# A chain of four networks in one program: value products of the last attention in column tiles, probabilities turned inside V's product, and the router's mean in column tiles

## The chip, the cores and the metric

The kernel runs on one core of one Trainium2 chip. The core has a matrix engine (PE, with its weight loads shown apart as PEld), a vector engine (DVE), a scalar engine (ACT), a general one (POOL) and SP, which here only issues transfers. Each engine works through its own list of instructions in order and waits on semaphores for the others. The metric is the device time of one execution in microseconds; three runs of the kernel before gave 366.67, 365.13 and 364.26, median 365.13.

## The reference

128 nodes with 768 features go through four layers, each a graph network and a feed-forward part. The change lies in the last feed-forward part, a small transformer block with a router. What matters of it, with x of 128 x 768 (here B = 1, N = 128):

```python
HEADS = 12; HD = 64; RHD = 512; RANK = 256
e = _gelu(_ln(x, r_ln_g, r_ln_b) @ r_in_w.T + r_in_b)
g = jnp.mean(e[:, RESERVE:, :], axis=1, keepdims=True)
f = jnp.concatenate([e, jnp.broadcast_to(g, e.shape)], axis=-1)
h1 = _gelu(f @ r_o1_w.T + r_o1_b)
h2 = _gelu(h1 @ r_o2_w.T + r_o2_b)
logits = (h2 @ r_o3_w.T + r_o3_b).reshape(B, N, BS, 2)
...
xa = _ln(x, ln1_g, ln1_b)
q = (xa @ wq.T + bq).reshape(B, N, HEADS, HD).transpose(0, 2, 1, 3)
...
s = jax.nn.softmax(jnp.einsum('bhqd,bhkd->bhqk', q, k) / np.float32(np.sqrt(HD)), axis=-1)
o = jnp.einsum('bhqk,bhkd->bhqd', s, v).transpose(0, 2, 1, 3).reshape(B, N, DIM)
o = o @ wo.T + bo
h = x + bits[:, :, 0:1] * o
```

Each node's router input is its own 512 features beside the mean of all nodes (the first one left out), so r_o1 is a product over 1024, of which the second 512 are the same for every node. Everything is float32.

## The kernel before

The program is written engine by engine; the order on each engine is the order of the code, and semaphores (wait_ge, then_inc) tie the engines together. Weights come through a ring of eight slots of 128 x 4608, each a unit that SP loads ahead; all units of the last part (r_in, wq, r_o1, wk, wv, wo, down, up) are such units. PSUM is one tensor of eight banks of 512 columns; bank(n, w, off) names w columns of bank n.

A product on PE is mm(out, stationary, moving): the stationary operand (up to 128 x 128) is loaded as weights and the moving one is streamed. In float32 each product shows in the trace as two passes, each a weight load and a MATMUL; a transposition tr is one pass. With tile_position a product uses only some rows or columns of the array: (0, 32 t) or (0, 64 n) is a column tile, whose output lies in 32 or 64 of the 128 partitions of PSUM. Two places of the kernel before use column tiles: L1724 (four tiles of 32 columns) and L1841 (join_mlp, two of 49). The scores at L1908 use two row tiles, one for the even heads (features 0 to 63 of a chunk), one for the odd ones.

The last block on PE runs in this order. product_T multiplies transposed activations: for each output chunk o of 128 it adds products over the input chunks c, all at L1862. First r_in (stationary weights, moving xT), four output chunks, each passed by ACT through GELU into h1[:, 0:512] (features on partitions, nodes in columns). Then q's product. Meanwhile DVE sums h1 over the nodes into gmean, 128 x 4. Then r_o1: per output chunk four products with the nodes' chunks of h1 and four with a column of gmean that is broadcast over 128 columns (node_or_mean); outputs alternate between banks 6 and 7, chunk o from the third on waits for the GELU of chunk o - 2, which ACT writes to h1[:, 512:1024] (L673). Then k's product, r_o2, and V's product (L1918): first the wide half, columns 0 to 511, then the narrow one, 512 to 767, six chunks each; behind the first chunk stand the router's logits (L1902) and the twelve score products (L1908).

During V's product DVE takes the maxima of the scores by groups of four heads (L1292), ACT takes the exponentials of twelve heads (L684), and DVE scales each group with one over its sum (L1298), which gives p_ready 1, 2 and 3. POSITION orders the heads. Then PE turns the twelve 128 x 128 probability blocks into banks 4, 5 and 3 (L1927), ACT copies each group to h2 (L495, pT_ready), DVE adds the bias to all of V at once into g4 (L1302, v_ready) and makes the residual g3 (L1305). A head's value product (L1935) has 128 stationary columns, that is both heads of a chunk of V, so that half of each output is not used:

```python
last = mm(ps[:, h * P:(h + 1) * P], g4[:, (h // 2) * P:(h // 2 + 1) * P], h2[:, at * P:(at + 1) * P],
          start=True, stop=True)
```

Even heads are taken from partitions 0 to 63 of the output by ACT (L495), odd ones from 64 to 127 by DVE (L1310), each in two pieces, into xT. The output projection (L1946) waits for both engines' first pieces, later for the second ones. Behind it come the residual (L1313), statistics, and the rest of the block.

## Time and profile before

| | us |
|---|---|
| Median of three runs | 365.13 |
| Span of the profiled execution | 362.7 |
| PE busy | 349.9 |
| DVE busy | 180.6 |
| ACT busy | 66.3 |
| r_o1, from its first pass to the first of k's product | 7.14 |
| From the end of V's product to the output projection | 4.19 |

The span goes from the first to the last instruction; the run's time also has what lies around it. The chain that ended last follows the work back from the last instruction to whatever released it; PE makes 84% of it. In a timeline, rows of one line that follow each other are put together with a count, and the time of such a row goes from its first start to its last end, where the end of a MATMUL is modelled and includes the way out of the array; passes that follow each other start closer together than they last.

### The profile page before, as it was taken

How to read it: one execution, taken by the hardware profiler on the slowest of the kernel's cores; microseconds unless marked ns; L12 is line 12 of the kernel's file. 1: busy time of each engine (PE TensorE's matmuls, PEld its weight loads, DVE VectorE, ACT ScalarE, POOL GpSimd, SP SyncE). 2: the span in 40 equal slices, each digit the busy share in tenths (PEclk: the TensorE clock that was granted, in tenths of full speed). 3: DMA queues.
4: the chain of work that ended last, by engine and by line, in shares of the span. 5: the costliest groups of instructions: out<-in, count | busy, mean ns of one | idle time of the engine just before them, and what ended most of it. 6: DMA issues, size and time to landing. Idle time of an engine off the chain costs nothing.

```text
span 362.7 us, 4277 instructions
## 1 busy us (share of the span) xinstructions
PE 349.9 (96%) x1633; PEld 222.1 (61%) x1633; DVE 180.6 (50%) x547; ACT 66.3 (18%) x154; POOL 38.4 (11%) x62
## 2 busy tenths in 40 slices
PE   7999999999999999999899999999999799999997
PEld 3466666656565656655556556564555599967754
DVE  4846337485838475467644835325642301163441
ACT  2002101101011111012012220024133401064010
POOL 4900000010000002041040000041030100000000
PEclk9999999999999999999999999999999999999999
DMA  8999999998854949999985375794371600000001
GB/s 279 416 379 429 428 416 427 424 380 303 345 230 149 414 149 418 413 408 414 382 376 192 136 272 213 260 354 161 150 276 28 275 2 3 0 2 0 2 0 43
DMA packets 10502, 90.19 MB, mean 249 GB/s; under 512 B 2169, under 2 KB 2822, under 8 KB 6386
## 3 DMA queue, kind: packets, MB, share of 16 engines
q1 hardware_dynamic: 8238, 84.91, 59.2%
q0 software_dynamic: 848, 3.61, 2.9%
q10 hardware_dynamic: 1396, 1.40, 1.1%
q8 instruction: 13, 0.21, 0.2%
q14 instruction: 7, 0.06, 0.0%
HBM read 89.53 MB, written 0.39 MB: 248 GB/s over the span
## 4 chain that ended last, share of the span: by engine, by line
PE 84%; DVE 8%; DMA 3%; issue 1%; SPq 1%; ACT 1%; POOL 1%; DVEq 0%; ACTq 0%
PE ps L1491 15%; PE ps L1457 14%; PE ps L1862 8%; PE ps L1436 6%; PE ps L1664 4%; PE ps L1683 4%; DMA ring<-in_gat_w 3%; PE ps L1479 3%; PE ps L1774 2%; PE ps L1946 2%; PE ps L1918 2%; PE ps L1966 2%; PE ps L1557 2%; DVE stats L716 1%; PE ps L1498 1%; PE ps L1368 1%
## 5 line engine op out<-in xcount | busy, mean ns | idle before, releaser
L1457 PE MATMUL ps<-ring,xT 128*128 128x512 f32 (+1 forms) x168 | 56.6, 486 | 0.9 <-DMA ring<-in_gat_w 0.9
L1491 PE MATMUL ps<-ring,h 128*128 128x512 f32 (+1 forms) x168 | 55.6, 486 | 0.0
L1491 PEld LDWEIGHTS ps<-ring,h 128*128 128x128 f32 x168 | 31.2, 190 | 21.9 <-issue 20.1
L1457 PEld LDWEIGHTS ps<-ring,xT 128*128 128x128 f32 x168 | 30.8, 191 | 20.0 <-issue 16.9
L782 DVE CUSTOM_DVE_ANT_0 g<-h,avec 128x768 f32<-128x768 f32 x8 | 7.7, 959 | 35.9 <-ACT h L495 22.8
L495 ACT ACTIVATE h<-ps 128x768 f32<-128x768 f32 (+6 forms) x24 | 13.6, 577 | 60.2 <-PE ps L1457 16.2
L1436 PE MATMUL ps<-ring,xT 128*128 128x512 f32 (+1 forms) x72 | 24.0, 487 | 0.0
L870 DVE TENSOR_SCALAR ring<-ring,idxb,ewb 128x128 bf16<-128x128 bf16 x99 | 22.5, 309 | 0.0
L1368 PE MATMUL ps<-shiftm 128*128 128x512 bf16 x66 | 19.4, 418 | 3.1 <-POOL shiftm L386 2.1
L380 POOL TENSOR_TENSOR rstd<-var,mhalf 128x1 f32<-128x1 f32 x8 | 4.6, 579 | 144.1 <-DVE var L724 69.3
L1436 PEld LDWEIGHTS ps<-ring,xT 128*128 128x128 f32 x72 | 13.4, 190 | 9.0 <-issue 8.1
L1683 PE MATMUL ps<-ring,h 128*128 128x512 f32 (+1 forms) x48 | 16.4, 492 | 0.0
L1862 PE MATMUL ps<-g,ring 128*128 128x128 f32 x144 | 16.4, 275 | 0.0
L1862 PEld LDWEIGHTS ps<-g,ring 128*128 128x128 f32 x144 | 16.2, 192 | 0.0
L1664 PE MATMUL ps<-ring,xT 128*128 128x384 f32 x48 | 16.0, 488 | 0.0
L495 ACT ACTIVATE xT<-ps 128x256 f32<-128x256 f32 (+2 forms) x18 | 7.1, 395 | 39.9 <-PE ps L1384 28.1
L1368 PEld LDWEIGHTS ps<-shiftm 128*128 128x128 bf16 x66 | 6.5, 110 | 12.5 <-issue 4.5
L1683 PEld LDWEIGHTS ps<-ring,h 128*128 128x128 f32 x48 | 8.8, 190 | 6.5 <-issue 6.1
L920 DVE TENSOR_TENSOR x<-ps,xb 128x512 f32<-128x512 f32 (+1 forms) x8 | 4.4, 553 | 16.7 <-PE ps L1436 13.4
L536 ACT ACTIVATE g<-g 128x768 f32<-128x768 f32 x8 | 6.7, 843 | 31.7 <-DVE g L816 31.7
L527 ACT ACTIVATE att<-att,soft 128x128 f32<-128x128 f32 x9 | 3.6, 402 | 48.5 <-DVE soft L799 48.5
L1261 DVE TENSOR_TENSOR g<-ps,cols 128x768 f32<-128x768 f32 x2 | 1.9, 958 | 20.9 <-PE ps L1862 20.9
(394 smaller groups left out, 512.7 us busy)
## 6 DMA issues: line engine op xcount, KB each, us to landing
ring<-in_gat_w SPq DMA_DIRECT2D x15, 2304.0 KB, 11.3
avec<-in_gat_a SPq DMA_DIRECT2D x9, 768.0 KB, 10.2
ring<-in_l_w SPq DMA_DIRECT2D x3, 2304.0 KB, 15.6
ring<-in_gat_w SPq DMA_DIRECT2D x6, 384.0 KB, 6.4
ring<-in_l_w SPq DMA_DIRECT2D x2, 1152.0 KB, 12.8
ring<-in_l1f_w1a SPq DMA_DIRECT2D x1, 2304.0 KB, 12.9
ring<-in_l1f_w1b SPq DMA_DIRECT2D x1, 2304.0 KB, 9.8
ring<-in_l1f_w2a SPq DMA_DIRECT2D x1, 2304.0 KB, 11.1
```

Of the source, the lines that this page charges most:

```text
L495: return nc.scalar.activation(dst, src, ACT.Copy)
L782: link(nc.vector.tensor_tensor_reduce(g3[:], hp, avec[:, 0:D], 1.0, 0.0, ALU.mult, ALU.add, alpha[:, par, 0:1]))
L870: last_ = nc.vector.tensor_scalar(oh_src[:, 1 + k, e, :], iotab, idxb[:, 1, e:e + 1], ewb[:, k, e:e + 1], ALU.is_equal, ALU.mult)
L1368: mm(bank(spare), some[:, 0:P], some[:, 0:WIN], start=True, stop=True)
L1436: last = mm(ps[:, at + lo:at + hi], xT[:, c, :], w[:, c, lo:hi], start=(c == 0), stop=(c == C - 1))
L1457: last = mm(ps[:, at + lo:at + hi], xT[:, c, :], w[:, c, lo:hi], start=(c == 0), stop=(c == C - 1))
L1479: last = mm(ps[:, 6 * WIN + c * P:6 * WIN + (c + 1) * P], h1[:, par * D + c * P:par * D + (c + 1) * P], attnT[:, par, :], start=True, stop ...
L1491: last = mm(ps[:, 4 * WIN + lo:4 * WIN + hi], h2[:, par * D + c * P:par * D + (c + 1) * P], w[:, c, lo:hi], start=(n == 0 and c == 0), sto ...
L1557: last = mm(ps[:, 4 * WIN + lo:4 * WIN + hi], h2[:, D + c * P:D + (c + 1) * P], w[:, c, lo:hi], start=False, stop=(c == C - 1))
L1664: last_ = mm(bank(g, H0), xT[:, c, :], weights[:, c, lo:lo + H0], start=(c == 0), stop=(c == C - 1))
L1683: last_ = mm(ps[:, lo:hi], h2[:, g * H0 + c * P:g * H0 + (c + 1) * P], weights[:, 3 * (g % 2) + c, lo:hi], start=False, stop=(g == 3 and c ...
L1862: last_ = mm(to, weights[:, c, o * P:(o + 1) * P], operand(c), start=(c == 0), stop=(c == chunks - 1))
```

## The change

In the router's r_o1, the mean's product is no longer repeated for 128 columns in each of four output chunks. Four column tiles of 32 take one column of gmean each as stationary operand (broadcast over 32 columns), with 512 columns of r_o1's weights moving, into the four quarters of bank 0: tile t's rows all hold chunk t's share of the mean's row. ACT copies bank 0, scaled by 1/32, to h2[:, 0:512] (mean_rows), and per output chunk one product of mean_rows with ones adds the sum over all 128 partitions to the four node products.

In the attention, the twelve turns of probabilities move into V's product, four after the wide half, four in the middle of the narrow half, four after it. V's bias is added in two instructions, one per half, with the residual's g3 between them. A head's value product has 64 stationary columns, and the two heads of a chunk go to two column tiles, so that a chunk's output lies as the projection needs it, on 128 partitions. Three copies of 128 x 256 take the place of four of 64 partitions: ACT, DVE, ACT.

```diff
+        mean_rows = h2[:, 0:RHD]
...
@@ ACT
+            act.wait_ge(s("mean_ps"), 1)
+            nc.scalar.activation(mean_rows, bank(0), ACT.Copy, scale=1.0 / BIT).then_inc(s("mean_copied"), 1)
             for f in range(4):
                 act.wait_ge(s("ro1_ps"), f + 1)
...
             for g in range(3):
                 act.wait_ge(s("pT_ps"), g + 1)
                 copy(h2[:, g * 512:(g + 1) * 512], bank((4, 5, 3)[g])).then_inc(s("pT_ready"), 1)
-            o_ps = ps[:, 0:AH * P].rearrange("p (c b n) -> p c b n", b=2, n=P)
-            for n, (lo, hi) in enumerate(((0, 4), (4, C))):
+            for n in (0, 2):
                 act.wait_ge(s("oT_ps"), n + 1)
-                copy(xT[0:AD, lo:hi, :], o_ps[0:AD, lo:hi, 0, :]).then_inc(s("o_even_ready"), 1)
+                copy(xT[:, 2 * n:2 * n + 2, :], bank(n, 2 * P).rearrange("p (c n) -> p c n", n=P)) \
+                    .then_inc(s("o_outer_ready"), 1)
...
@@ DVE
-            dve.wait_ge(s("v_ps"), 1)
+            def heads_values(n):
+
+                lo, hi = HALVES[n]
+                dve.wait_ge(s("v_ps"), n + 1)
+                nc.vector.tensor_tensor(g4[:, lo:hi], ps[:, 6 * WIN + lo:6 * WIN + hi], avec[:, D + lo:D + hi], ALU.add) \
+                    .then_inc(s("v_ready"), 1)
+
             dve.wait_ge(s("in_bv"), 16)
-            nc.vector.tensor_tensor(g4[:], ps[:, 6 * WIN:6 * WIN + D], avec[:, D:2 * D], ALU.add).then_inc(s("v_ready"), 1)
-
+            heads_values(0)
             dve.wait_ge(s("in_bo"), 16)
             link(nc.vector.scalar_tensor_tensor(out=g3[:], in0=avec[:, 0:D], scalar=bit[:, 0:1], in1=xn[:], op0=ALU.mult,
                                                 op1=ALU.add))
-            o_ps = ps[:, 0:AH * P].rearrange("p (c b n) -> p c b n", b=2, n=P)
-            for n, (lo, hi) in enumerate(((0, 4), (4, C))):
-                dve.wait_ge(s("oT_ps"), n + 1)
-                nc.vector.tensor_copy(xT[AD:P, lo:hi, :], o_ps[AD:P, lo:hi, 1, :]).then_inc(s("o_odd_ready"), 1)
+            heads_values(1)
+            dve.wait_ge(s("oT_ps"), 2)
+            nc.vector.tensor_copy(xT[:, 2:4, :], bank(1, 2 * P).rearrange("p (c n) -> p c n", n=P)) \
+                .then_inc(s("o_inner_ready"), 1)
...
@@ PE
-            product_T(unit(U_RO1, "r_o1", "p (c n) -> p c n", c=8), 6, 4, node_or_mean, "ro1_ps", emptied="h1T_ready")
+            w = unit(U_RO1, "r_o1", "p (c n) -> p c n", c=8)
+            for t in range(4):
+                last = mm(ps[t * BIT:(t + 1) * BIT, 0:RHD], gmean[:, t:t + 1].broadcast_to([P, BIT]), w[:, 4 + t, :],
+                          start=True, stop=True, tile_position=(0, t * BIT))
+            last.then_inc(s("mean_ps"), 1)
+            for o in range(4):
+                if o >= 2:
+                    pe.wait_ge(s("h1T_ready"), o - 1)
+                for c in range(4):
+                    mm(bank(6 + o % 2, P), w[:, c, o * P:(o + 1) * P], h1[:, c * P:(c + 1) * P], start=(c == 0), stop=False)
+                if o == 0:
+                    pe.wait_ge(s("mean_copied"), 1)
+                mm(bank(6 + o % 2, P), mean_rows[:, o * P:(o + 1) * P], ones[:], start=False, stop=True) \
+                    .then_inc(s("ro1_ps"), 1)
...
+            def turn_probabilities(g):
+
+                pe.wait_ge(s("p_ready"), g + 1)
+                for h in range(4):
+                    last_ = tr(bank((4, 5, 3)[g], P, h * P), h1[:, (4 * g + h) * P:(4 * g + h + 1) * P], ident)
+                last_.then_inc(s("pT_ps"), 1)
...
                     if lo == 0 and c == 0:
                         scores()
+                    if lo > 0 and c == 2:
+                        turn_probabilities(1)
+                last.then_inc(s("v_ps"), 1)
+                if lo == 0:
+                    turn_probabilities(0)
+            turn_probabilities(2)
...
+            def out_at(c):
+
+                return bank(c // 2, P, c % 2 * P)
+
+            def heads_out(c):
+
+                for half in range(2):
+                    at = POSITION[2 * c + half]
+                    last_ = mm(out_at(c)[half * AD:(half + 1) * AD],
+                               g4[:, c * P + half * AD:c * P + (half + 1) * AD], h2[:, at * P:(at + 1) * P],
+                               start=True, stop=True, tile_position=(0, half * AD))
+                return last_
 
             pe.wait_ge(s("v_ready"), 1)
+            pe.wait_ge(s("pT_ready"), 2)
+            for c in range(C):
+                if c == 4:
+                    pe.wait_ge(s("v_ready"), 2)
+                    pe.wait_ge(s("pT_ready"), 3)
+                last = heads_out(c)
+                if c % 2:
                     last.then_inc(s("oT_ps"), 1)
             wait_unit(pe, U_O)
...
                     if lo == 0 and c in (0, 4):
-                        pe.wait_ge(s("o_even_ready"), 1 + c // 4)
-                        pe.wait_ge(s("o_odd_ready"), 1 + c // 4)
+                        pe.wait_ge(s("o_outer_ready"), 1 + c // 4)
+                    if lo == 0 and c == 2:
+                        pe.wait_ge(s("o_inner_ready"), 1)
```

The order on PE at r_o1, before. A row is a line, the operation, out<-in, the output's shape and a count; in the brackets stand the semaphores that it waits for. The names in it: h is h1 (the nodes' features), cells is gmean, ring the weights.

```order
L1862 MATMUL ps<-h,ring 128x128 [waits gmean_ready,slot3_in]
L1862 MATMUL ps<-h,ring 128x128 x3
L1862 MATMUL ps<-cells,ring 128x128 x4
L1862 MATMUL ps<-h,ring 128x128 x4
L1862 MATMUL ps<-cells,ring 128x128 x4
L1862 MATMUL ps<-h,ring 128x128 [waits h1T_ready]
L1862 MATMUL ps<-h,ring 128x128 x3
L1862 MATMUL ps<-cells,ring 128x128 x4
L1862 MATMUL ps<-h,ring 128x128 [waits h1T_ready]
L1862 MATMUL ps<-h,ring 128x128 x3
L1862 MATMUL ps<-cells,ring 128x128 x4
```

After the change, the same place; here h at L1907 is h2 (mean_rows).

```order
L1897 MATMUL ps<-ring,cells 32x512 [waits gmean_ready,slot3_in]
L1897 MATMUL ps<-ring,cells 32x512 x3
L1904 MATMUL ps<-h,ring 128x128 x4
L1907 MATMUL ps<-ones,h 128x128 [waits mean_copied]
L1904 MATMUL ps<-h,ring 128x128 x4
L1907 MATMUL ps<-ones,h 128x128
L1904 MATMUL ps<-h,ring 128x128 [waits h1T_ready]
L1904 MATMUL ps<-h,ring 128x128 x3
L1907 MATMUL ps<-ones,h 128x128
L1904 MATMUL ps<-h,ring 128x128 [waits h1T_ready]
L1904 MATMUL ps<-h,ring 128x128 x3
L1907 MATMUL ps<-ones,h 128x128
```

The sixteen products with the mean are gone from between the node products; the four with 512 columns stand ahead of them, and one product per output chunk behind.

The order on PE from the end of V's wide half through the value products, before: h at L1927 is h1 (probabilities), at L1935 it is h2 (turned probabilities), and g is g1 or g4 (V).

```order
L1918 MATMUL ps<-ring,g 128x256 x6
L1927 MATMUL ps<-shiftm,h 128x128 [waits p_ready]
L1927 MATMUL ps<-shiftm,h 128x128 x3
L1927 MATMUL ps<-shiftm,h 128x128 [waits p_ready]
L1927 MATMUL ps<-shiftm,h 128x128 x3
L1927 MATMUL ps<-shiftm,h 128x128 [waits p_ready]
L1927 MATMUL ps<-shiftm,h 128x128 x3
L1935 MATMUL ps<-h,g 128x128 [waits pT_ready,v_ready]
L1935 MATMUL ps<-h,g 128x128 x3
L1935 MATMUL ps<-h,g 128x128 [waits pT_ready]
L1935 MATMUL ps<-h,g 128x128 x3
L1935 MATMUL ps<-h,g 128x128 [waits pT_ready]
```

After the change:

```order
L1934 MATMUL ps<-shiftm,h 128x128 [waits p_ready]
L1934 MATMUL ps<-shiftm,h 128x128 x3
L1942 MATMUL ps<-ring,g 128x256 x3
L1934 MATMUL ps<-shiftm,h 128x128 [waits p_ready]
L1934 MATMUL ps<-shiftm,h 128x128 x3
L1942 MATMUL ps<-ring,g 128x256 x3
L1934 MATMUL ps<-shiftm,h 128x128 [waits p_ready]
L1934 MATMUL ps<-shiftm,h 128x128 x3
L1961 MATMUL ps<-h,g 64x128 [waits pT_ready,v_ready]
L1961 MATMUL ps<-h,g 64x128 x7
L1961 MATMUL ps<-h,g 64x128 [waits pT_ready,v_ready]
L1961 MATMUL ps<-h,g 64x128 x3
```

The twelve turns, which stood behind V's narrow half, stand in three places, and the value products wait twice instead of three times, for two signals each.

The order on DVE at the same place, before and then after the change (g is g4, then g3; cells holds sums and bits).

```order
L1298 TENSOR_TENSOR h<-h,cells 128x512 [waits dve_step]
L1302 TENSOR_TENSOR g<-ps,avec 128x768 [waits in_bv,v_ps]
L1305 SCALAR_TENSOR_TENSOR g<-avec,cells,xn 128x768 [waits in_bo]
L1310 COPY xT<-ps 64x512 [waits oT_ps,dve_step]
L1310 COPY xT<-ps 64x256 [waits oT_ps]
L1313 SCALAR_TENSOR_TENSOR g<-ps,cells,g 128x512 [waits wo_ps]
```

```order
L1302 TENSOR_TENSOR h<-h,cells 128x512 [waits dve_step]
L1308 TENSOR_TENSOR g<-ps,avec 128x512 [waits v_ps,in_bv]
L1314 SCALAR_TENSOR_TENSOR g<-avec,cells,xn 128x768 [waits in_bo]
L1308 TENSOR_TENSOR g<-ps,avec 128x256 [waits v_ps,dve_step]
L1318 COPY xT<-ps 128x256 [waits oT_ps]
L1322 SCALAR_TENSOR_TENSOR g<-ps,cells,g 128x512 [waits wo_ps]
```

V's bias is two instructions with g3 between them, and one copy of 128 partitions stands where two of 64 stood.

## Rows read from the trace of the kernel before

**Rows 1.** The page: span, busy us of each engine, PE's granted clock by slices.

```profile
span 362.7 us, 4277 instructions
...
PE 349.9 (96%) x1633; PEld 222.1 (61%) x1633; DVE 180.6 (50%) x547; ACT 66.3 (18%) x154; POOL 38.4 (11%) x62
...
PEclk9999999999999999999999999999999999999999
```

**Rows 2.** Chain that ended last, from 299.9 us: start us, us, what.

```profile
299.90 17.42 PE ps L1862 x156
...
318.52 1.54 PE ps L1908 x24
320.06 7.08 PE ps L1918 x22
327.14 1.31 PE ps L1927 x12
328.45 2.82 PE ps L1935 x24
...
331.33 7.99 PE ps L1946 x24
...
352.35 7.76 PE ps L1436 x24
```

**Rows 3.** The same chain, earlier: passes of 384 columns, and L1841's second piece.

```profile
207.39 3.87 PE ps L1664 x12
...
283.21 1.45 PE ps L1841 x8
```

**Rows 4.** Timeline of PE at the two column-tiled lines: start us, us, line, count.

```profile
234.85 2.16 PE L1724 MATMUL ps<-ring,h 128*32 128x192 f32 x48
...
279.40 2.79 PE L1841 MATMUL ps<-ring,h 128*49 128x384 f32 x16
```

**Rows 5.** Timeline of PE's weight loads at L1841.

```profile
279.40 0.17 PEld L1841 LDWEIGHTS ps<-ring,h 128*49 128x49 f32 x4 [0.33 <-issue]
279.77 0.13 PEld L1841 LDWEIGHTS ps<-ring,h 128*49 128x49 f32 x2 [0.19 <-issue]
280.09 0.13 PEld L1841 LDWEIGHTS ps<-ring,h 128*49 128x49 f32 x2 [0.19 <-issue]
```

**Rows 6.** Timeline of PE over r_o1: the first piece of each kind.

```profile
300.19 1.06 PE L1862 MATMUL ps<-h,ring 128*128 128x128 f32 x8
301.08 1.06 PE L1862 MATMUL ps<-cells,ring 128*128 128x128 f32 x8
```

**Rows 7.** Groups by line and shape, 225 to 363 us: busy us, mean ns.

```profile
L495 ACT ACTIVATE xT<-ps 128x256 f32<-128x256 f32 x8 | 3.1, 384 | 18.7 <-PE ps L1384 10.3 <-PE ps L1951 6.8 <-PE ps L1828 1.6
...
L495 ACT ACTIVATE h<-ps 128x512 f32<-128x512 f32 x3 | 1.6, 598 | 2.6 <-PE ps L1927 2.6
```

**Rows 8.** Timeline of ACT: first GELU of r_o1, end of the last exponential.

```profile
302.17 0.37 ACT L673 ACTIVATE h<-ps,cols 128x128 f32<-128x128 f32 x1 [9.46 <-PE ps L1862]
...
324.70 0.27 ACT L684 ACTIVATION_READ_ACCUMULATOR h<-ps,cells 128x1 f32 x1
```

**Rows 9.** Timeline of DVE: first and last of three scalings, g3, copies.

```profile
322.42 0.69 DVE L1298 TENSOR_TENSOR h<-h,cells 128x512 f32<-128x512 f32 x1
...
325.21 0.69 DVE L1298 TENSOR_TENSOR h<-h,cells 128x512 f32<-128x512 f32 x1
...
328.06 1.01 DVE L1305 SCALAR_TENSOR_TENSOR g<-avec,cells,xn 128x768 f32<-128x768 f32 x1
330.49 1.25 DVE L1310 COPY xT<-ps 64x512 f32<-64x512 f32 x2 [1.42 <-PE ps L1935]
```

**Rows 10.** Instructions of L1841 and L1862: ns min/median/max, first and last start.

```profile
L1841 PEld LDWEIGHTS ps<-ring,h x24: 120/124/124, 279.4 to 283.8; 128*49 128x49 f32 x24
L1841 PE MATMUL ps<-ring,h x24: 486/486/524, 279.4 to 284.1; 128*49 128x384 f32 x24
...
L1862 PEld LDWEIGHTS ps<-g,ring x144: 191/192/192, 292.0 to 315.2; 128*128 128x128 f32 x144
```

More of the change, by code:

```diff
@@ L1921, in _ @@
                         scores()
-            last.then_inc(s("v_ps"), 1)
-            pT_banks = (4, 5, 3)
-            for g in range(3):
-                pe.wait_ge(s("p_ready"), g + 1)
-                for h in range(4):
-                    last = tr(bank(pT_banks[g], P, h * P), h1[:, (4 * g + h) * P:(4 * g + h + 1) * P], ident)
-                last.then_inc(s("pT_ps"), 1)
-            pe.wait_ge(s("v_ready"), 1)
-            for at in range(AH):
-                h = POSITION.index(at)
-                if at % 4 == 0:
-                    pe.wait_ge(s("pT_ready"), at // 4 + 1)
-                last = mm(ps[:, h * P:(h + 1) * P], g4[:, (h // 2) * P:(h // 2 + 1) * P], h2[:, at * P:(at + 1) * P],
-                          start=True, stop=True)
-                if at in (7, 11):
+                    if lo > 0 and c == 2:
[13 more added lines that the diff above has]
+                return last_
+            pe.wait_ge(s("v_ready"), 1)
+            pe.wait_ge(s("pT_ready"), 2)
[5 more added lines that the diff above has]
+                if c % 2:
                     last.then_inc(s("oT_ps"), 1)
```

2 lines of the change are left out of this document (removed).

## The prediction

> **What bounds the kernel now.** I read the page's shares first: PE is busy 96% of the span, and PEclk stays at 9 in all forty slices, which is the 2.4 GHz level [rows 1]. Then the chain that ended last, from 299.9 us on: one PE line begins where the one before ends, to within 0.06 us, and no transfer and no other engine stands between them up to the end of the output projection [rows 2]. So both places of the change lie on the chain, and a microsecond of PE saved there is a microsecond of the span, as long as no copy becomes late.
>
> Three prices come out of the chain. A float32 product takes two passes, each a weight load and a MATMUL. A pass with 128 moving columns costs 17.42 / 156 = 0.1117 us, a transposition (one pass) 1.31 / 12 = 0.109 [rows 2]. A pass with 384 columns costs 3.87 / 12 = 0.3225 us [rows 3], or 0.84 ns per column, which makes 0.43 for 512 and 0.215 for 256. Check: 12 x 0.43 + 12 x 0.215 = 7.74, and the last product takes 7.76 [rows 2].
>
> **Column tiles in the trace of before.** Two lines already use them. L1841 has two tiles of 49 columns: 16 passes of 384 columns take 2.79 us from the first start to the modelled end [rows 4]. Alone they would take 16 x 0.3225 = 5.2. The weight loads show the pattern: two of them every 0.32 us, one full-width slot [rows 5]. L1724 has four tiles of 32 columns: 48 passes of 192 columns in 2.16 us [rows 4], where 12 sets of 0.161 make 1.94 and 48 single passes would make 7.7. So both two and four tiles run side by side, and a set costs as much as one pass.
>
> Going in and out of tiles is not free. Scores (row tiles, 12 pairs, 128 columns) take 1.54 us where 12 x 0.1117 = 1.34, so 0.20 to enter. The V product behind them takes 7.08, where 10 wide and 12 narrow passes make 6.88, so 0.20 to leave [rows 2]. L1841's second piece, 8 passes or 4 sets, takes 1.45 instead of 1.29: 0.16 to enter with narrow tiles [rows 3].
>
> **The change part by part.**
>
> *Router's mean.* Removed: 16 products against the broadcast mean, 32 passes in four pieces of 8 [rows 6], 32 x 0.1117 = 3.57 us. Added: four tiles with 512 columns, two sets of 0.43 = 0.86; entering 0.15 and leaving 0.20; four products of the copied mean rows with the ones, 8 x 0.1117 = 0.89. Together 2.10, so 1.47 is saved. Bounds: the two sets cost 0.86 if four tiles run side by side (L1724) and 8 x 0.43 = 3.44 if they don't; I take 0.86, since L1724 has the same number of tiles and the same 32 columns, and only its moving width differs.
>
> New on ACT is one copy of 128x512 from PSUM; the nearest row says 598 ns [rows 7]. PE waits for it before the ones' product of the first output chunk. From the start of the tiles' last set: 0.60 until its modelled end (a MATMUL of 384 lasts 486 ns [rows 10], 0.165 more than its slot, so 0.43 + 0.165), 0.04 hand-over, 0.60 copy, 0.04 back: 1.28. PE meanwhile streams 0.43, leaves the tiles 0.20 and does eight node passes 0.89: 1.52. The copy is hidden with 0.24 to spare. If it isn't, each tenth is a tenth of the span. Behind the copy on ACT stand the four GELUs of r_o1; the first is wanted by the third chunk, ten passes (1.12) after its product ended, and takes 0.37 [rows 8].
>
> *Value products.* Before, from 328.45 to the start of L1946 at 331.33: 2.88 us for 24 passes, with a small wait at the front and one for the copies at the end [rows 2]. After: 12 sets of two tiles with 64 weight columns. Bounds for a set: 0.109 (the transposition's slot) below, 2 x 0.1117 = 0.223 above if the pair takes turns. No row has two column tiles of 64 columns and a moving width of 128. The nearest are the scores, paired by rows at that width, and L1841, paired by columns at three times the width; in both a pair costs one slot, so I take 0.1117. 12 x 0.1117 + 0.17 to enter = 1.51; leaving falls into L1946, which takes 7.99 now against 7.76 for an unhindered product [rows 2], so it already pays about what leaving costs. Saved: 2.88 - 1.51 = 1.37.
>
> *Transpositions inside V.* Nothing is removed: 12 x 0.109 stay on PE in three groups of four. Their purpose is the copies behind them. I laid the new order on the clock of before (as if the router's part were unchanged). V's wide half ends about 324.45 (320.06 + 5 x 2 x 0.43, and some delay at its start); the first group needs p_ready 1, given when DVE's first scaling ends at 323.1; the three scalings stand 1.39 us apart [rows 9]. So it doesn't wait, and ends at 324.9. Three narrow chunks (6 x 0.215) end at 326.2, the second group (p_ready 2: 324.5) at 326.6, three more chunks at 327.9, the third group (p_ready 3: 325.9) at 328.35. ACT is through with the exponentials at 324.97 [rows 8], copies the first group by 325.6, the second by 327.4, and the third (ready 0.2 after its last slot) by 329.2. DVE adds bias to V's wide half from 325.9 to 326.6 (0.69, as its other pass over 128x512), makes g3 (1.01) until 327.7, and adds bias to the narrow half (ready at about 328.1) by 328.6 [rows 9].
>
> PE's first four head pairs need V's wide half (326.6) and copies 1 and 2 (327.4), and run from 328.5 to 329.4; the last two need the narrow half (328.6) and copy 3 (329.2), and run to 329.85. The margin is 0.2 us, the smallest of this part; without it each tenth that ACT is late is a tenth of the span. Results leave in three copies of 128x256, 0.38 each on ACT [rows 7] and about as much on DVE: the first, behind copy 3, is done at 329.6, the second on DVE at about 330.0, the third on ACT at 330.5. The output projection takes them at 329.85, four wide passes later (331.7) and eight later (333.4). None is late. The half-height copies of before, DVE's two of them at 330.49 [rows 9], which ended after the last value product, disappear from the path.
>
> **The sum.** 1.47 + 1.37 = 2.84 us. The profiled execution's span is 362.7; the runs have a median of 365.13, 2.4 more, which I take as what lies around the span and leave unchanged. So the span becomes 359.8 and the time 362.3 us, 0.8% less. A difference of about 1% is what a measurement of this kernel can tell from none: its three times lie between 364.26 and 366.67.
>
> **The rivals.**
>
> A. The pair of 64-column tiles takes turns at 128 columns: a set costs 0.223, the value products 2.7 + 0.2, and their part is nothing. Only the mean pays: 365.13 - 1.47 = 363.7. For it: no row has this form, and each set must load 128 weight columns within 0.11 us. Against it: the scores load two sets of 128 columns per slot and lose nothing.
>
> B. A new wait takes part of the gain: the mean's copy (margin 0.24) or the third copy of the probabilities (0.2). If ACT needs half a microsecond more at both, 0.6 comes back: 362.9. For it: both margins are small; against it: ACT has no other work at the mean's place, where it was idle for 9.46 us before the first GELU [rows 8].
>
> C. Slower: column tiles take turns at both places, and a pass's weight load isn't covered by the pass before. A load lasts 124 ns for 49 columns and 192 for 128 [rows 10], so about 137 for 64 and 110 for 32. Values: 24 x (0.137 + 0.112) + 0.17 = 6.15, 3.3 more than now; mean: 8 x (0.110 + 0.43) + 0.35 + 0.89 = 5.56, 2.0 more; in all 370.4. Turns alone already raise the mean's two sets from 0.86 to 3.44, and the whole is 1.1 us slower (366.2). Each part alone turns to a loss once a set of four costs over 1.17 us, a pair over 0.226. Against it: at L1841's start four loads lie within 0.17 us [rows 5], so the second pair loads while the first pair's matmuls, 486 to 524 ns long [rows 10], run. The Trainium skill states this rule ("TensorE: Matmul & The Clock Gate", Part 3, The mechanism): a weight load overlaps running matmuls only if its row group differs, which it doesn't among column tiles; by that rule the time would be C's. The trace disagrees: at L1841 and L1724 all passes use the same 128 rows, and a set still costs one slot.
>
> D. More than the sum: entering and leaving cost nothing (L1927 follows L1918 without a gap) and a pair's slot is 0.109, 0.55 us more: 361.7.
>
> **How the numbers follow.** The forecast 0.66, A 0.10, B 0.12, C 0.04, D 0.08. The likeliest is 362.3; A and B reach up to 363.7, D down to 361.7, and the median of a few runs of this kernel may lie half a microsecond off: 361.0 to 363.9. Faster by over 1% means below 361.5: a fifth of the forecast (scatter) and half of D, 0.18; C holds 0.04, of which a quarter (turns with covered loads) is within 1%, so slower has 0.03; the rest, 0.79, is within 1%.
>
> **What would show it.** In the profile after, the chain should stay on PE. The line of the four-tile mean should have 8 passes, whose weight loads come in two groups of four, 0.43 to 0.46 us apart; the stretch from the end of q's product to the first K pass should shrink from 64 x 0.1117 = 7.15 to about 5.7; the value products' 24 passes should take about 1.5 in the chain, and the output projection should start 0.05 us behind them without a wait. PE idle before the ones' product (on ACT's copy) shows B, as does idle before the fifth head pair; pairs 0.22 apart show A. I would be wrong most likely in the price of entering and leaving tiles, which I know only as a difference of sums.

## The result, and the profile after

The changed kernel takes 362.44 us (median of six runs, 361.21 to 363.22), the kernel before beside it 364.84 (six runs, 364.26 to 366.67). The ratio is 0.9927, with a 95% interval of 0.9904 to 0.995: a gain of 0.7%, about what was forecast, and within the 1% at which the chances were drawn. The profiled execution took 362.13 us with a span of 360.3; before, the span was 362.7 [rows 1].

The page of the changed kernel: the span, and busy us of each engine.

```profile
span 360.3 us, 4241 instructions
...
PE 346.4 (96%) x1612; PEld 217.9 (60%) x1617; DVE 180.2 (50%) x547; ACT 66.8 (19%) x155; POOL 38.3 (11%) x62
```

The chain that ended last, from r_o1 on: start us, us, what. L1897 is the four-tile mean, L1904 the node products, L1907 the products of the mean rows with ones, L1942 V, L1934 the turns, L1961 the value products, L1983 the output projection; L1871 is product_T.

```profile
300.93 0.99 PE ps L1897 x8
301.92 1.09 PE ps L1904 x8
303.01 0.22 PE ps L1907 x2
303.24 0.89 PE ps L1904 x8
...
306.59 9.83 PE ps L1871 x88
...
319.15 4.49 PE ps L1942 x10
323.64 0.44 PE ps L1934 x4
324.08 1.30 PE ps L1942 x6
...
327.55 1.46 PE ps L1961 x24
329.01 7.95 PE ps L1983 x24
```

One PE line begins where the one before ends, as in [rows 2]. No row of ACT or DVE has come in between, so none of the new copies is late. The value products take 1.46 us where L1935 took 2.82. The same stretch as a timeline of PE (start us, time to the modelled end of the last pass, line, stationary and moving operand, shape, count):

```profile
300.86 1.06 PE L1897 MATMUL ps<-ring,cells 128*32 128x512 f32 x8
301.85 1.16 PE L1904 MATMUL ps<-h,ring 128*128 128x128 f32 x8
...
306.42 8.20 PE L1871 MATMUL ps<-g,ring 128*128 128x128 f32 x72
...
319.08 4.56 PE L1942 MATMUL ps<-ring,g 128*128 128x512 f32 x10
...
327.48 1.53 PE L1961 MATMUL ps<-h,g 128*64 128x128 f32 x24
328.94 8.01 PE L1983 MATMUL ps<-ring,xT 128*128 128x512 f32 x24
```

Two stretches can be read from first starts, which are not modelled, and they serve as yardsticks below. The **r_o1 stretch**, from its first pass to k's first, is 300.86 to 306.42, 5.56 us; before it was 7.14. The **V stretch**, from V's restart behind the scores to the output projection, is 319.08 to 328.94, 9.86 us; before it ran from 319.99 to 331.33, 11.34. That is 1.58 and 1.48 us less. Of the first, 0.09 is given back ahead of it: in the trace of single instructions the first tile's pass starts 0.20 us behind q's last pass, where passes that follow each other at this width stand 0.11 apart. Net 1.49 + 1.48 = 2.97 us, against 2.84 in the sum. From the two spans only 2.4 is gone: r_in, which lies ahead of all that the change touches, began 0.58 us later in this execution (287.29, before 286.71), and 2.97 - 0.58 = 2.39. The experiments come back to this.

### The profile page after: what moved, and what is told of

Read it like the earlier page. It is cut to its first block, busy times and chain, and to the rows that moved or that the text cites. A ratio compares the mean times of both kernels' runs of the same rounds, so it can differ in the third digit from the quotient of the medians.

```text
span 360.3 us, 4241 instructions
## 1 busy us (share of the span) xinstructions
PE 346.4 (96%) x1612; PEld 217.9 (60%) x1617; DVE 180.2 (50%) x547; ACT 66.8 (19%) x155; POOL 38.3 (11%) x62
## 4 chain that ended last, share of the span: by engine, by line
PE 80%; DMA 10%; DVE 5%; SPq 2%; issue 1%; ACT 1%; POOL 1%; DVEq 0%; ACTq 0%
PE ps L1500 15%; PE ps L1466 14%; PE ps L1445 7%; PE ps L1871 7%; DMA ring<-in_l_wu 6%; PE ps L1673 4%; PE ps L1692 4%; DMA ring<-in_gat_w 3%; PE ps L1488 3%; PE ps L1783 2%; PE ps L1983 2%; PE ps L1942 2%; PE ps L2003 2%; PE ps L1566 2%; DVE stats L720 2%; PE ps L1507 1%
## 5 line engine op out<-in xcount | busy, mean ns | idle before, releaser
L1466 PEld LDWEIGHTS ps<-ring,xT 128*128 128x128 f32 x168 | 30.8, 191 | 20.3 <-issue 16.9
L1377 PE MATMUL ps<-shiftm 128*128 128x512 bf16 x61 | 17.8, 412 | 3.6 <-POOL shiftm L388 2.1
L1445 PEld LDWEIGHTS ps<-ring,xT 128*128 128x128 f32 x72 | 13.4, 190 | 9.0 <-issue 8.1
L1871 PE MATMUL ps<-g,ring 128*128 128x128 f32 x144 | 16.4, 275 | 0.0
L1871 PEld LDWEIGHTS ps<-g,ring 128*128 128x128 f32 x144 | 16.2, 192 | 0.0
L497 ACT ACTIVATE xT<-ps 128x256 f32<-128x256 f32 x18 | 6.9, 383 | 38.5 <-PE ps L1393 27.9
L1673 PEld LDWEIGHTS ps<-ring,xT 128*128 128x128 f32 x48 | 8.9, 190 | 5.6
```

Source lines behind the costliest of these rows:

```text
L497: return nc.scalar.activation(dst, src, ACT.Copy)
L1377: mm(bank(spare), some[:, 0:P], some[:, 0:WIN], start=True, stop=True)
L1445: last = mm(ps[:, at + lo:at + hi], xT[:, c, :], w[:, c, lo:hi], start=(c == 0), stop=(c == C - 1))
L1466: last = mm(ps[:, at + lo:at + hi], xT[:, c, :], w[:, c, lo:hi], start=(c == 0), stop=(c == C - 1))
L1673: last_ = mm(bank(g, H0), xT[:, c, :], weights[:, c, lo:lo + H0], start=(c == 0), stop=(c == C - 1))
L1871: last_ = mm(to, weights[:, c, o * P:(o + 1) * P], operand(c), start=(c == 0), stop=(c == chunks - 1))
```

## The experiments

e1 to e8 were to tell which part earns what, and why; w1 to w4 came of the scatter in their times. Line numbers differ by a few from kernel to kernel. Kernels with a single run are read by the two stretches, not by the time.

### e1 and e2: each part alone

e1 has the mean in column tiles and the attention of before:

```diff
-            product_T(unit(U_RO1, "r_o1", "p (c n) -> p c n", c=8), 6, 4, node_or_mean, "ro1_ps", emptied="h1T_ready")
+            w = unit(U_RO1, "r_o1", "p (c n) -> p c n", c=8)
+            for t in range(4):
+                last = mm(ps[t * BIT:(t + 1) * BIT, 0:RHD], gmean[:, t:t + 1].broadcast_to([P, BIT]), w[:, 4 + t, :],
+                          start=True, stop=True, tile_position=(0, t * BIT))
...
```

> The kernel before with the router's mean in four column tiles and nothing else. My theory: the two parts of the change are independent, each pays what its own stretch of PE shows. From the first pass of r_o1 to the first of k's product 5.56 us as after (7.14 before); from V's wide half (first pass behind the scores) to the output projection 11.34 as before; time 1.5 us below the kernel before, about 363.3. Rival (the parts share a cover, so that one alone pays little): less than 1 us gained.

e2 has the attention of the change and the mean of before (the same lines the other way round):

```diff
-            for t in range(4):
-                last = mm(ps[t * BIT:(t + 1) * BIT, 0:RHD], gmean[:, t:t + 1].broadcast_to([P, BIT]), w[:, 4 + t, :],
-                          start=True, stop=True, tile_position=(0, t * BIT))
...
+            product_T(unit(U_RO1, "r_o1", "p (c n) -> p c n", c=8), 6, 4, node_or_mean, "ro1_ps", emptied="h1T_ready")
```

> The kernel after with the router's mean as before (16 products with the broadcast mean). My theory: r_o1 takes 7.14 again; from V's wide half to the output projection 9.86 as after (11.34 before); time 1.5 us below the kernel before, about 363.4. Rival (shared cover): under 1 us gained, or PE idle before the fifth pair of heads.

e1 took 363.13 us (eleven runs), ratio 0.9944 with an interval of 0.9923 to 0.9966; e2 363.47 (nine runs), 0.9948 with 0.9925 to 0.9972. In e1 the r_o1 stretch is 301.54 to 307.10, 5.56 us as after, and the V stretch 11.34 as before. In e2 the r_o1 stretch is 7.15 as before, and the V stretch 319.89 to 329.74, 9.85 as after. PE's timeline of e2 at the value products:

```profile
328.28 1.53 PE L1950 MATMUL ps<-h,g 128*64 128x128 f32 x24
329.74 1.55 PE L1972 MATMUL ps<-ring,xT 128*128 128x512 f32 x3
```

By the stretches the two parts do not touch each other, and each pays half. The times of all runs are too wide to say as much; w1 to w4 come back to them.

### e3: the turns behind V, as before

```diff
-                    if lo > 0 and c == 2:
-                        turn_probabilities(1)
...
-                if lo == 0:
-                    turn_probabilities(0)
-            turn_probabilities(2)
+            for g in range(3):
+                turn_probabilities(g)
```

> The kernel after with all twelve turns behind V's narrow half again; the pairs in column tiles stay. My theory: the turns' new place is what keeps ACT's copies off the path. With the turns at the end, copies 1 and 2 (0.60 each) end 1.84 us after V, the turns on PE after 1.31, so PE waits about 0.5 us before the first pair; from V's wide half to the output projection 10.35 (9.86 after). Rival 1: the place of the turns is worth nothing, 9.9. Rival 2: it carries the gain, 11.3.

The one run took 363.65 us. The V stretch is 320.17 to 330.48, 10.31 us, as expected. PE's timeline; the bracket says how long PE sat idle ahead of the row, and what it waited for:

```profile
329.02 1.53 PE L1958 MATMUL ps<-h,g 128*64 128x128 f32 x24 [0.39 <-ACT h L497]
```

The pairs are as quick as after, but wait 0.39 us for ACT's copy of the probabilities. With pairs, moving the turns into V is worth 10.31 - 9.86 = 0.45 us, though it takes no instruction away.

### e4: the turns inside V, the value products full-width

```diff
-                               g4[:, c * P + half * AD:c * P + (half + 1) * AD], h2[:, at * P:(at + 1) * P],
-                               start=True, stop=True, tile_position=(0, half * AD))
...
+                last = mm(ps[:, h * P:(h + 1) * P], g4[:, (h // 2) * P:(h // 2 + 1) * P], h2[:, at * P:(at + 1) * P],
+                          start=True, stop=True)
```

> The kernel after with full-width value products (128 stationary columns, 24 passes one after another, copies in four half-height pieces as before), the turns inside V. My theory: the pairs carry most of the attention's gain: 24 x 0.1117 = 2.68 for the products, 11.1 from V's wide half to the output projection (9.86 after, 11.34 before). Rival (the pair in two column tiles gains nothing at 128 moving columns, the earlier copies do): 9.9 to 10.2.

With them come back the four half-height copies of before. The one run took 364.31 us. PE's timeline:

```profile
328.33 2.84 PE L1961 MATMUL ps<-h,g 128*128 128x128 f32 x24
331.16 1.10 PE L1972 MATMUL ps<-ring,xT 128*128 128x512 f32 x2
```

The V stretch is 320.03 to 331.16, 11.13 us: 0.21 less than before from the place of the turns, and the pairs, with their own copies, are worth the other 1.27. Together with e3: without pairs the place is worth 0.21, with them 0.45. The pairs need the first two copies of probabilities at their front, where the full-width order needs one, so with the turns behind V they wait 0.39 us there (e3); in the kernel before, the twelve turns took 328.36 - 326.98 = 1.38 us to the first value product, only 0.07 more than their slots of 0.109.

### e5: all even heads, then all odd ones

This asks what lets two tiles run side by side: that they use different columns, or that they stand next to each other in the program.

```diff
-            for c in range(C):
...
-                last = heads_out(c)
+            for half in range(2):
+                for c in range(C):
...
+                    last = mm(out_at(c)[half * AD:(half + 1) * AD],
+                              g4[:, c * P + half * AD:c * P + (half + 1) * AD], h2[:, at * P:(at + 1) * P],
+                              start=True, stop=True, tile_position=(0, half * AD))
```

> The kernel after with the value products in another order: all six even heads (tile 0), then all six odd ones (tile 1); the waits for V's narrow half and the third copy move ahead of the first. My theory: passes start in the order of the program, and only neighbours in it run side by side, so 24 passes of about 0.105 follow each other: 2.6 us for the products instead of 1.46, and a wait of 0.7 for the third copy ahead of them; from V's wide half to the output projection 11.7. Rival (PE takes later passes for the other tile ahead): products 1.5, stretch 10.6.

The one run took 364.88 us. PE's timeline:

```profile
329.25 2.42 PE L1962 MATMUL ps<-h,g 128*64 128x128 f32 x24 [0.78 <-ACT h L497]
331.61 1.13 PE L1975 MATMUL ps<-ring,xT 128*128 128x512 f32 x2
```

The same 24 passes take 2.36 us from first to next start, instead of 1.46. In the trace of single instructions the passes stand 0.109 us apart, one after another; only at the border do the last four even passes (330.15 to 330.48) and the first four odd ones (330.16 to 330.53) run side by side. The first odd pass starts at 330.16, while three even ones that stand ahead of it in the program start only at 330.26 to 330.48: PE does reach ahead for the other tile, against my theory, but here by no more than three passes. So two tiles share a slot only if their passes are near neighbours in PE's program. The idle time ahead is that of a wait for all three copies, which this order needs at the front; with it the V stretch is 331.61 - 320.01 = 11.60 us, 11.7 expected.

### e6: the mean's four products in one tile

All four tiles write to the first 32 rows of the bank and add up there; ACT's copy and the ones' products then take 32 rows.

```diff
-                last = mm(ps[t * BIT:(t + 1) * BIT, 0:RHD], gmean[:, t:t + 1].broadcast_to([P, BIT]), w[:, 4 + t, :],
-                          start=True, stop=True, tile_position=(0, t * BIT))
+                last = mm(ps[0:BIT, 0:RHD], gmean[:, t:t + 1].broadcast_to([P, BIT]), w[:, 4 + t, :],
+                          start=(t == 0), stop=(t == 3), tile_position=(0, 0))
...
-                mm(bank(6 + o % 2, P), mean_rows[:, o * P:(o + 1) * P], ones[:], start=False, stop=True) \
+                mm(bank(6 + o % 2, P), mean_rows[0:BIT, o * P:(o + 1) * P], ones[0:BIT, :], start=False, stop=True) \
```

> The kernel after with the mean's four products of 512 columns all in one tile of 32 columns, added up there (the products with ones then take 32 rows). My theory: without the side-by-side running each of the eight passes costs its full 0.43, 2.6 us more than two sets: from r_o1's first pass to k's 8.1 instead of 5.56, more than the 7.14 of before; time 365.0, no better than before. Rival (the gain comes from not repeating the mean, whatever the tiles): 5.6.

e6 took 366.07 us (ten runs), ratio 1.0033 with an interval of 1.0009 to 1.0057. The r_o1 stretch is 301.84 to 311.39, 9.55 us, and here I missed: 1.45 more than expected. PE's timeline:

```profile
301.84 3.62 PE L1897 MATMUL ps<-ring,cells 128*32 128x512 f32 x8
305.39 1.16 PE L1904 MATMUL ps<-h,ring 128*128 128x128 f32 x8
306.48 0.48 PE L1907 MATMUL ps<-ones,h 32*128 32x128 f32 x2
306.89 1.16 PE L1904 MATMUL ps<-h,ring 128*128 128x128 f32 x8
```

The first row is as expected: eight passes that no longer run side by side take 305.39 - 301.84 = 3.55 us, where they took 0.99. The miss is in the rows below. A chunk of ten passes takes 306.89 - 305.39 = 1.50 us, where it takes ten slots, 1.12, after the change. The ones' product now has 32 rows, and its shape reads 32*128. My reading is that it is a row tile by that, so that each of the four chunks goes into tiles and out again, 0.38 us each time, 1.5 in all. What speaks for it: its first pass starts 0.205 us behind the node pass before it, as the first tile of the mean does behind q's last pass. A 32-row product that is not taken for a row tile was not tried.

### e7: the mean as a bias

The mean's row is the same for all nodes, so it need not be added on PE at all. In e7 the mean rows are turned, one transposition per chunk, DVE sums the four tiles' shares and adds r_o1's bias, and the GELU takes the sum as its bias; the ones' products are gone. The third output chunk goes to bank 0, so that only the fourth waits for a GELU.

```diff
-                mm(bank(6 + o % 2, P), mean_rows[:, o * P:(o + 1) * P], ones[:], start=False, stop=True) \
-                    .then_inc(s("ro1_ps"), 1)
...
+                    for k in range(4):
+                        last = tr(bank(1, P, k * P), mean_rows[:, k * P:(k + 1) * P], ident)
...
+            shares = bank(1).rearrange("p (o t n) -> p o t n", o=4, n=BIT)[:, :, :, 0]
+            link(nc.vector.tensor_reduce(cell("mean_part", 4), shares, AX.X, ALU.add))
+            nc.vector.tensor_tensor(cell("ro1_bias", 4), cell("mean_part", 4), col("r_o1_b"), ALU.add) \
```

> The kernel after with the mean's share turned instead of multiplied: four transpositions of the copied rows (one pass of 0.109 each) take the place of four products with ones (8 passes of 0.1117); DVE adds the four shares and r_o1's bias, and ACT's GELU takes that as its bias; the third output chunk goes to bank 0. My theory: 0.89 - 0.44 = 0.45 us less on PE, 5.1 from r_o1's first pass to k's, 362.0, with the first GELU later but not waited for. Rival: the first GELU, which now waits for the turns and DVE, is late for the fourth output chunk, and PE waits there: 5.5 or more.

```profile
300.00 1.07 PE L1904 MATMUL ps<-ring,cells 128*32 128x512 f32 x8
300.99 1.16 PE L1911 MATMUL ps<-h,ring 128*128 128x128 f32 x8
301.99 0.60 PE L1917 MATMUL ps<-shiftm,h 128*128 128x128 f32 x4
302.42 2.84 PE L1911 MATMUL ps<-h,ring 128*128 128x128 f32 x24
305.10 1.61 PE L1878 MATMUL ps<-g,ring 128*128 128x128 f32 x13
```

In this timeline of PE the stretch is 300.00 to 305.10, 5.10 us as expected, 0.46 less than after: four turns instead of eight passes, and no wait. The time was 361.20 us (six runs), ratio 0.9908 with an interval of 0.988 to 0.9937. That overlaps the change's 0.9904 to 0.995, so the time does not tell the two apart.

### e8: a full-width product between the pairs

```diff
                 if c % 2:
                     last.then_inc(s("oT_ps"), 1)
+                if c < 5:
+                    stay_warm(1, 5)
```

stay_warm(1, 5) is one bf16 product of 512 columns into a bank that nobody reads.

> The kernel after with one full-width bfloat16 product of 512 columns (0.215 us) behind each of the first five pairs of heads, so that PE leaves the column tiles and enters them again five times. My theory: leaving costs about 0.1 to 0.2 and entering about 0.15 each time, whatever the stretch in between: 5 x (0.215 + 0.30) = 2.6 more, 4.0 us from the first value product to the output projection (1.46 after). Rival (the price lies in the length of the stretch or in its first loads only): 5 x 0.215, 2.5 us.

The one run took 363.51 us. PE's timeline, from the third such product on, and the projection:

```profile
328.26 0.39 PE L1377 MATMUL ps<-shiftm 128*128 128x512 bf16 x1
328.58 0.44 PE L1961 MATMUL ps<-h,g 128*64 128x128 f32 x4
...
329.27 0.44 PE L1961 MATMUL ps<-h,g 128*64 128x128 f32 x4
...
330.33 1.55 PE L1985 MATMUL ps<-ring,xT 128*128 128x512 f32 x3
```

A pair with the dummy behind it comes every 0.69 us. From the first pair's start at 326.50 the projection is 3.83 us away, where it is 1.46 after the change: (3.83 - 1.46) / 5 = 0.47 per dummy. Such a dummy has a slot of 0.22 us (four in a row take 1.04 elsewhere in this kernel's traces, one 0.38), so leaving the tiles and entering them again costs 0.25 us, a little under the 0.30 that I expected. That the dummy is bfloat16 is not the price: among full-width passes of this trace a bfloat16 one starts 0.112 us behind a float32 one of 128 columns (at 245.68 us), and a float32 one 0.056 us behind a bfloat16 one of 128 (at 255.80 us), in both cases a plain slot. The Trainium skill ("TensorEngine Tiling (Array Packing)", Tiling Modes, Key Properties) says that a change of the tiling mode, not of the tile alone, drains the engine; e6 and e8 agree in that each change costs time, 0.38 and 0.25 us.

### w1 to w4: what scatters the time

The profiles of e3 to e6 had a mean granted clock of 0.995, the others 1.000, and their r_o1 began at 301.79 to 301.94 us; in the others it began between 299.9 and 300.9, but for e1 (301.54). Where it goes is seen in windows (us, width, PE busy with instructions, granted clock, transfers' share, GB/s), here of e6:

```profile
286.00:287.00 1.00, 0.36 (x3) 1.00 0.92 393
287.00:288.00 1.00, 1.00 (x8) 0.69 0.60 246
288.00:289.00 1.00, 1.00 (x7) 0.50 0.03 12
289.00:290.00 1.00, 1.00 (x7) 0.50 0.00 0
290.00:291.00 1.00, 1.00 (x7) 0.60 0.00 0
291.00:292.00 1.00, 1.00 (x11) 1.00 0.00 0
```

The clock stands at 0.50, the 1.2 GHz level, from about 287.4 to 290.8 us. PE had been idle until 286.64. PE's timeline at r_in, of e6, then of the changed kernel, then of the kernel before:

```profile
286.64 7.22 PE L1871 MATMUL ps<-xT,ring 128*128 128x128 f32 x48 [2.08 <-ACT xT L514]
```

```profile
287.29 5.60 PE L1871 MATMUL ps<-xT,ring 128*128 128x128 f32 x48 [2.08 <-ACT xT L514]
```

```profile
286.71 5.60 PE L1862 MATMUL ps<-xT,ring 128*128 128x128 f32 x48 [2.08 <-ACT xT L512]
```

All three wait 2.08 us for ACT; in the first the clock then falls and the same 48 passes take 1.62 us more, in the others it doesn't. w1 to w3 fill that idle with seven dummies: in the kernel before, the changed one, and e7. w4 is the changed kernel once more.

```diff
             join_mlp(range(4, C)).then_inc(s("mlp_ps"), 1)
+            stay_warm(7, 3)
             wait_unit(pe, U_RIN)
```

> The kernel before, with seven dummy bf16 products of 512 columns (0.215 us each) put into the 2.08 us in which PE waits for ACT ahead of r_in. Why: the profiles of e3 to e6 have a mean granted clock of 0.995, and in them the clock stands at 0.50, the 1.2 GHz level, for about 3 us behind this idle (287 to 290.5 us), so that r_in's 48 passes take 7.22 us, against 5.60 where the clock stays at 1.00. The runs of before in the last two calls split the same way: 21 of 36 have a mean clock of 1.000 and a median of 364.6, 15 have 0.995 and a median of about 366.1. Theory (the idle makes the clock fall): no run shows 0.995 any more, the median is 364.6 and the scatter goes from 3 us to about 1. Rival 1 (something else makes it fall): about two runs in five still show 0.995, and the median stays at 364.8 to 365.8. Rival 2 (the dummies are late): r_in starts later, each tenth is a tenth of the span; seven dummies end 1.5 us behind the column tiles, 0.6 before r_in is wanted, so I expect none.

> The same seven dummies in the changed kernel. Theory: no run at 0.995, median 362.0 (after's four runs at 1.000: 361.21 to 362.74, median 362.04). With the scatter gone, the difference to the kernel before with the same dummies should be the one that the two stretches give, 1.49 + 1.48 = 2.97 us, so 361.6 against 364.6; if instead it is 2.4 to 2.5, as the medians gave, half a microsecond is lost somewhere between the stretches and the time, and the two stretches do not say all.

> The variant with the mean as a bias (e7), with the same seven dummies. Theory: no run at 0.995, median 361.1 (e7's four runs at 1.000: 360.89 to 361.31), which is 0.46 below the changed kernel with the dummies and 3.4 below the kernel before with them. Rival (the mean's stretch is not all that e7 changed, its smaller bank traffic costs elsewhere): no difference from the changed kernel with the dummies.

> The changed kernel as it is, once more, on the same chip. Theory: its runs split into two groups, mean granted clock 1.000 at about 362.0 and 0.995 at about 363.2 to 363.5, and within a group it stands about 2.9 us below the kernel before; the median of all depends on how many fall into each. Rival (the scatter has nothing to do with the clock ahead of r_in): no split by clock, times spread evenly.

The timeline of PE in w2, where the idle was (the trace has six of the seven dummies):

```profile
285.13 1.46 PE L1377 MATMUL ps<-shiftm 128*128 128x512 bf16 x6 [0.16 <-issue]
287.05 2.13 PE L1871 MATMUL ps<-xT,ring 128*128 128x128 f32 x17 [0.46 <-ACT xT L514]
```

| kernel | runs | median us | lowest to highest | runs at 0.995 |
|---|---|---|---|---|
| before (with w1 to w4) | 17 | 365.91 | 364.45 to 367.05 | 11 |
| w1, before with dummies | 12 | 364.60 | 364.06 to 364.89 | 0 |
| w4, the change again | 6 | 362.29 | 361.00 to 363.11 | 2 |
| w2, the change with dummies | 6 | 361.56 | 361.12 to 361.88 | 0 |
| w3, e7 with dummies | 6 | 361.46 | 360.55 to 362.05 | 0 |

No run with dummies has a clock under 1.000, and the scatter of before falls from 2.6 us to 0.8. Over all experiments the kernel before has 27 runs at 1.000 with a median of 364.6 and 26 at 0.995 with 366.1; only one run of the first group (366.26) lies among the second. w4's six split as its theory said, but a little lower: four at 1.000 with a median of 361.8, two at 0.995 with 363.0. With the runs of the result the changed kernel has 8 at 362.0 and 4 at 363.2. Between w1 and w2, where the clock no longer decides, the change is worth 364.60 - 361.56 = 3.04 us, and no run of the one reaches the other's. The stretches said 2.97: nothing is lost on the way. The 2.4 between the first medians mixed runs of both clocks, as far as they are known: two of the changed kernel's six were at 0.995, and the six of the kernel before have no clock on record. Within a clock, without dummies, the medians stand 2.6 (at 1.000) and 2.9 us apart (at 0.995), from eight and four runs of the changed kernel; what is missing there to 2.97 is within their scatter of 1.7 us, and was not followed further.

The same split serves e1 and e2. At 1.000 (0.999 taken with it) the kernel before stands at 364.63 (nine runs beside them), e1 at 363.09 (eight) and e2 at 363.12 (six), 1.54 and 1.51 less, as their stretches say. But the clock is not all of the scatter: at 1.000 e1 still goes from 362.46 to 364.41, and its profile, late at r_o1 (301.54), has a clock of 1.000. What delays it there was not tried; its chain ahead of r_o1 has transfers of avec (4.5% up to 300 us).

w3 is a miss by its time: 0.10 us below w2, where I expected 0.46. Its r_o1 stretch is 300.94 to 306.04, 5.10 us, as in e7, so the gain is there on PE, and it is kept: from r_o1's first pass to the output projection w3 takes 27.62 us, w2 28.08. Its r_o1 starts 0.33 us later than w2's (300.61), and its runs spread over 1.5 us although the clock is 1.000 in all of them. In its chain ahead of 300 us the transfers of avec hold 7.2%, in w2's those of a gate's weights 4.3%. That arrivals of transfers differ is read there; that they alone take up the 0.36 was not tried.

## Why the prediction was right

**The bound.** Both places lay on the chain of PE, and what PE saved there left the span. w1 against w2 shows it: 3.04 us of time for 2.97 in the two stretches.

**The mean, term by term.** Forecast -1.47, measured -1.49. Two sets of four tiles were taken at 0.43 each, entering and leaving at 0.35, forty other passes at 0.1117. The stretch of 5.56 with the 0.09 ahead of it, less 0.86 and 4.47, leaves 0.32 for entering and leaving, or 0.27 if a set is taken at the 0.453 that lie between the two sets. L1724's 32-column tiles were the right row to go by, also at another width.

**The value products.** Forecast -1.37, measured -1.48 for the whole V stretch. The sets of two passes stand 0.110 us apart (0.1117 was taken), and 24 passes cost 1.46 (1.51 was taken). The rest of the difference lies in the old side: 2.88 was read from the chain, which counts from an end, and the starts give 331.33 - 328.36 = 2.97.

**The margins.** Both held, but both were closer than worked out, the second by nearly all of it. ACT in the changed kernel: the mean's copy, then the last copy of the probabilities and the first one of the results (the bracket is ACT's idle time):

```profile
301.99 0.60 ACT L674 ACTIVATE h<-ps 128x512 f32<-128x512 f32 x1 [8.70 <-PE ps L1897]
...
327.58 0.60 ACT L497 ACTIVATE h<-ps 128x512 f32<-128x512 f32 x1 [1.14 <-PE ps L1934]
328.18 0.38 ACT L497 ACTIVATE xT<-ps 128x256 f32<-128x256 f32 x1
```

The mean's copy ends at 302.59, and the ones' product's first pass starts at 302.85, when the node passes are through: 0.26 between the two, of which some 0.04 are the hand-over, against 0.24 forecast. But what waits for the copy is the pass's weight load, one slot ahead of it:

```profile
302.74 0.30 PEld L1907 LDWEIGHTS ps<-ones,h 128*128 128x128 f32 x2
```

That leaves 0.15 us, 0.11 without the hand-over. The same holds for the fifth head pair: its pass starts at 328.40, 0.22 behind the end of the third probabilities' copy at 328.18 (0.2 forecast), but its first load stands at 328.30. PE's wait for that copy ends only at 328.22, and the pair's second load comes at 328.33, 0.03 later than the spacing of the loads before it; the passes keep their 0.110. So a copy later by some hundredths of a microsecond would have begun to cost time, where I had 0.2 to spare. My sum left out that the load goes ahead of its pass.

The narrow half's bias on DVE ends at 327.64, 8.56 us behind V's restart (forecast 328.6 on the clock of before, 8.61 behind it):

```profile
324.90 0.68 DVE L1308 TENSOR_TENSOR g<-ps,avec 128x512 f32<-128x512 f32 x1
...
327.22 0.42 DVE L1308 TENSOR_TENSOR g<-ps,avec 128x256 f32<-128x256 f32 x1 [0.70 <-PE ps L1942]
```

**The rivals.** A (pairs take turns) is refuted by 0.110 us between sets, not 0.22; e5 shows that this price is real once the order is another. B (ACT is late) is refuted by the missing wait, though narrowly; e3 shows what a late copy costs there, 0.39. D (entering and leaving for nothing) is refuted by 0.32 at the mean and by e8. C, the rival with the sign turned, needed tiles that take turns, which the 0.110 refutes, and loads that wait for running passes. The instructions of L1897 (ns min/median/max, first and last start us):

```profile
L1897 PEld LDWEIGHTS ps<-ring,cells x8: 105/106/108, 300.9 to 300.9; 128*32 128x32 f32 x8
L1897 PE MATMUL ps<-ring,cells x8: 592/604/616, 300.9 to 301.3; 128*32 128x512 f32 x8
```

All eight loads start within 0.1 us, while the second set's passes start only at 301.3: the second set is loaded under the first one's running passes, in the same 128 rows. The spacing agrees: a load of 0.105 that waited for passes of 0.43 would put the sets 0.53 apart, and they stand 0.453 apart. The rule of the Trainium skill ("TensorE: Matmul & The Clock Gate", Part 3, The mechanism), that a load overlaps running matmuls only if its row group differs, is not what these rows show. It also corrects a detail of mine: I expected the loads in two groups 0.43 to 0.46 us apart. It is the passes that come so (0.453 apart), the loads do not wait for them.

**What was wrong but cancelled.** I took 2.4 us as what lies around the span. In every run with a span on record it is 1.75 to 1.94 (362.13 against 360.3 after). The other 0.6 lay between the profiled execution and the median of three runs, whose clocks are not on record. The time was forecast as a median less 2.84, so the mistake cancels as far as the runs of the two kernels hold both clocks in a like share. The difference itself was sized well: 2.84 against the 2.97 of the stretches. That the time came within 0.14 us (362.3 against 362.44) is partly luck: the median of the kernel before fell from 365.13 to 364.84 with three more runs, and the medians lie only 2.40 apart; 0.29 too high a start and 0.44 too large a gain nearly cancel.

## What to carry to other kernels

A product that uses half or a quarter of the array's columns is worth putting into column tiles even for two sets, if its tiles follow each other directly in the program and no full-width product, nor one with a short contraction, stands between them; count about 0.3 us for going in and out. Read what an edit is worth from first starts around its own stretch, and look where PE idles ahead of it: a clock that falls there in some executions moves the median by about as much as one part of this change. Moving work that is not removed pays when it gives the copy behind it time to hide.

## What the hardware showed that I had not expected

- Behind a wait of 2.08 us on PE the granted clock fell to the 1.2 GHz level for some 3 us (in the traces of e3 to e6); by their mean clock of 0.995, 26 of 53 executions of the kernel before had the same, at 1.5 us each. With the wait filled, down to idle stretches of 0.16 and 0.46 us, none of 24 executions did. Seven dummy products are thus worth 1.3 us in the median of before (365.91, with 11 of 17 runs at 0.995, against 364.60), nearly as much as one part of the change.
- A product with 32 stationary rows costs 0.38 us more than one with 128 among full-width products, as if it were a row tile, though it was not asked for as one (e6).
- Column tiles run side by side only as near neighbours in the program: 0.110 us for a set of two passes, 0.109 for a single pass when the even heads stand first. At the border there an odd pass started ahead of three even ones that the program has before it (e5).
- Four tiles of 32 columns at 512 moving columns take 0.453 us per set, 3.8 times as quick as four passes of 0.43; the loads of the next set lie under the running passes.
